# Gates, lengths and the odd value tile's Silu at other places of ScalarE's slot, and the odd value projection ahead of the odd tile's transposition

## The chip, the cores and the metric

One core of a Trainium2 chip runs the whole program. The metric is the device time of one execution in microseconds (us), median of the runs. The engines are TensorE (matmuls; PE, with its weight loads as PEld), VectorE (DVE), ScalarE (ACT), GpSimd (POOL) and SyncE (SP), which only issues DMAs. Each engine runs its own instruction list in order, and they are tied together by semaphores that count up.

## The reference

Four layers over x of 8 x 256 tokens of width 128, each `x = x + f(layernorm(x))`. The first is a gated delta rule with 16 heads, the second a matmul with the signs of a weight, the third a causal attention with 4 key heads, the fourth a mixture of 8 experts with the top 2. The change lies in the first:

```python
q = _causal_conv_silu(x @ Wq.T, conv_q); k = _causal_conv_silu(x @ Wk.T, conv_k)
v = _causal_conv_silu(x @ Wv.T, conv_v)                 # 4 taps, then Silu
q = _l2_norm(q); k = _l2_norm(k)
alpha = exp(-exp(A_log) * softplus(x @ Wa.T + dt_bias)); beta = 2 * sigmoid(x @ Wb.T)
# per token: S = a*(S - b*k k^T S) + k v^T ;  o = S^T q
o = _rms_norm(o).reshape(Bx, Tx, H * DV);  return o @ Wo.T
```

## The kernel before

The recurrence is done in blocks: for each pair of heads and each pair of batches (512 tokens) the decay factors, the products of keys with keys and queries, the inverse of a triangular matrix, and two block solves. There are NN = 32 such steps n (4 parts p of two batches, 8 pairs of heads each). A part needs three things once: the norm of its x, its gates (alpha and beta, from Abs, Exp and Ln on ScalarE) and its lengths (the logarithms of the norms of q and k, split into three bf16 rows for the decay matmul).

The work is laid out by hand as a software pipeline. The loop `for s in range(LAG, NN + LAG + 3)` with LAG = 9 is written out once per engine. One turn s is a slot, and it works on several steps at once: k (projection, taps and Silu of the key and query tiles 2s and 2s+1, only in slots s < 32), g = s - 9 (decays, grams, value tiles 2g and 2g+1), i = s - 10 and j = s - 11 (the two halves of the inverse, then the solves and the output), w = s - 12 (output projection). The last slots also begin the attention. Each engine's order inside a slot is the order of the lines, so a wait holds all that stands behind it on that engine.

The names used here, with the lines of the profile:
- `decay(g, i)` (L531 to L542) writes exponents into bank 2; ScalarE's `exp(g, i)` (L1066) makes `et` of them; `gram(g, i)` (L565) multiplies keys and queries into banks 3 and 1; VectorE's `am` (L1369, L1372) multiplies both, two instructions a gram. A gram must wait until the products of the gram before it are made.
- `inv_a` (L592), `inv_b` (L603), `inv_c` (L610) and `inv_d` (L617) are the inverse's matmuls; `inv_p` (L1394), `inv_y` (L1400, with transpositions L1403 and L1406) and `inv_0` (L1383 to L1390) its steps on VectorE; `inv_n` (L1077), `inv_yf` (L1072, L1073) and `inv_o` (L1083) those on ScalarE. `inv_0` waits for both copies of `inv_yf`.
- `vproj(v)` (L498) projects value tile v, the even one into bank 0, the odd one into bank 2; `vcopy` (L1004, L1009) copies it out, `vconv` (L1293) adds three taps, `vsilu` (L1013) applies Silu, `vtr` (L511) transposes it into bank 0, `vV` (L1023) copies that into V. The even projection waits for the odd tile's vV, since both use bank 0.
- `solve1` (L629), `solve2` (L637), `solve3` (L645) and `out` (L661, L663) are the solves; `u1` (L1089) and `u2` (L1093) copy their results; `ot` (L1099, L1100) squares and copies the outputs. `solve1(j)` waits for `inv_yf(j)` and `inv_o(j)`.
- `kcopy` (L980, L983), `kconv` (L1293), `ksilu` (L990), `ksq` (L996) and `ksel` (L477) make the keys and queries and their squared lengths; `squares` (L672), `rms` (L1416, L1420) and `wout` (L688, L1432) finish a step.
- `gates1` and `gates2` (ScalarE L1028 to L1040, VectorE L1308 to L1332) and `lengths1` to `lengths4` (ScalarE L1044 to L1057, VectorE L1334 to L1356) are the steps of a part. `GAP` says in which slot a norm, a gate matmul or a length matmul is added.
- `exp_ahead` (L1016) is an Exp over one column that nobody reads; in front of it the compiler puts the load of ScalarE's Exp table.
- SyncE: `factors(p)` writes the factors of a part to DRAM, `spread(n)` reads them back over the partitions, `blocks(n)` sends the diagonal blocks through DRAM to GpSimd, `rows(n)` copies the rows of the decay matmul. GpSimd: `substitute` (L1743 to L1751), `scaled` (L1759), a power (L1771).

Of the kernel before, what the change touches and what calls it, by code (L numbers as in the profile page):

```python
# [17 lines left out]
NG = H // GH  # L18
# [3 lines left out]
LAG = 9  # L22
# [7 lines left out]
def program(nc, x_d, wqkv_d, conv_d, wab_d, gate_d, wo_d, sgn_d, awq_d, awk_d, awv_d, awo_d,  # L30
            wr_d, wg_d, wu_d, wd_d, acst_d, ident_d, bmask_d, emask_d, lmask_d, sel_d, reset_d, tri_d, amask_d, out_d):
    with ExitStack() as ctx:
        def sb(name, shape, dt=F32):
            return ctx.enter_context(nc.sbuf_tensor(name, shape, dt))
# [45 lines left out]
        ones = sb("ones", [128, 32])  # L80
        spare = sb("spare", [128, 2])
        ST = sb("ST", [128, 8, 32])
# [151 lines left out]
        for p in range(NP):  # L234
# [5 lines left out]
            if p < NP - 1:  # L240
                GAP[NG * p + 21] = ("norm", ("sg", p))
                GAP[NG * p + 22] = ("signed", p)
        GAP[NN + LAG - 1] = ("norm", ("at", 0))

        def gap(s, kind):
            k, v = GAP[s] if s in GAP else (None, None)
            return v if k == kind else None
# [168 lines left out]
        def _(e):  # L416
# [479 lines left out]
            for s in range(LAG, NN + LAG + 3):  # L896
# [11 lines left out]
                if has_w: squares(w)  # L908
                more(s, 2)
                if has_g: gram(g, 1)  # L910
                if gap(s, "lengths") is not None: lengths(gap(s, "lengths"))
                if gap(s, "gates") is not None: gates(s // NG)
                if gap(s, "norm") is not None: norm(gap(s, "norm"), bank[0], s_vV, 2 * g - 1)
                if gap(s, "signed") is not None: signed_mm(gap(s, "signed"), bank[0], s_vV, 2 * g - 1)
                if has_j: inv_b(j, 1)
                elif j < 0: fill(4)
                more(s, 3)
                if has_g: decay(g, 2)
                if has_g: gram(g, 2)
                if 0 < g < NN: vtr(2 * g - 1)  # L920
                if has_j: inv_c(j)
                elif j < 0: fill(2)
                more(s, 4)
                if has_g: vproj(2 * g)
                if has_j: inv_d(j)
                elif j < 0: fill(2)
                if has_g: vproj(2 * g + 1)
                if has_k and s % NG == NG - 1: ksel(2 * s)
# [36 lines left out]
        def _(e):  # L965
# [32 lines left out]
            def vcopy(v):  # L998
                e.wait_ge(s_vproj, v + 1)
                if v >= 2:  # L1000
                    e.wait_ge(s_vfin, v - 1)
                else:
                    e.wait_ge(s_kfin, NK0)
                e.activation(vy[:, v % 2, :, 3:259], vbank(v)[:, :].rearrange("p (b t) -> p b t", b=2), ACT.Copy).then_inc(s_vcopy, 1)  # L1004
                if v >= 2:
                    e.wait_ge(s_vtr, v - 1)
                else:
                    e.wait_ge(s_ksel, NK0)
                e.activation(vc[:, v % 2, :], vbank(v)[:, :], ACT.Copy, scale=conv[:, 16 + v % 16, 3:4]).then_inc(s_vtap, 1)  # L1009
# [5 lines left out]
            def exp_ahead():  # L1015
                e.activation(spare[:, 1:2], spare[:, 0:1], ACT.Exp)  # L1016

            def vV(v):
# [173 lines left out]
            for s in range(LAG, NN + LAG + 3):  # L1192
# [7 lines left out]
                if g == NN: vV(2 * g - 1)  # L1200
                if has_l: lengths2(p)
                if has_g: exp(g, 1)
                more(s, 0)
                more(s, 1)
                if gap(s, "norm") is not None: norm(gap(s, "norm"))
                if has_l: lengths3(p)
                more(s, 2)
                if has_g: exp(g, 2)
                more(s, 3)
                if has_k: ksilu(2 * s)  # L1210
                if has_k: ksilu(2 * s + 1)
                if 0 < g < NN: vV(2 * g - 1)
                if has_j: inv_n(j)
                if has_j: inv_yf(j)
                more(s, 4)
                if gap(s, "gates") is not None: gates1(s // NG)
                if has_k: ksq(2 * s)
                if has_j: inv_o(j)
                if has_e: ksq(2 * s + 1)
                if has_g: vcopy(2 * g)  # L1220
                if has_k and not has_e: ksq(2 * s + 1)
                if has_g: vcopy(2 * g + 1)
                if has_e: lengths1(s // NG)
                if has_j: u1(j)
                if gap(s, "gates") is not None: gates2(s // NG)
                more(s, 5)
                if has_p: kcopy(2 * s + 2)
                more(s, 6)
                if has_g: vsilu(2 * g)
                if has_p: kcopy(2 * s + 3)  # L1230
                if has_j: u2(j)
                more(s, 7)
                if has_j and j >= NN - 3: ot(j, 0)
                if has_g: vsilu(2 * g + 1)
                if 0 <= g < NN - 1: exp_ahead()
                if has_g: vV(2 * g)
# [10 lines left out]
        def _(e):  # L1247
# [408 lines left out]
            for s in range(LAG, NN + LAG + 3):  # L1656
# [6 lines left out]
                if has_k: kconv(2 * s)  # L1663
                if has_l: lengths2(p)
                if has_j: inv_p(j, 1)
# [3 lines left out]
                more(s, 1)  # L1669
                if has_l: lengths3(p)  # L1670
                if has_k: kconv(2 * s + 1, [0])
# [3 lines left out]
                if has_g: am(g, 3)  # L1675
                if has_l: lengths4(p)
                if gap(s, "gates") is not None: gates1(s // NG)
# [6 lines left out]
                if has_g: am(g, 4)  # L1684
                if has_g: am(g, 5)
                more(s, 4)
                if has_i: inv_0(i)
                if has_w: wout(w, 0)
                if has_e: lengths1(s // NG)
# [7 lines left out]
                more(s, 7)  # L1697
                if LAG < s < NN and s % NG > 2: gates2(s // NG, s % NG - 3)
                if gap(s + 1, "norm") is not None: norm(gap(s + 1, "norm"))
# [173 lines left out]
```

## Time and profile before

| | us |
|---|---|
| median of 3 runs | 1714.56 |
| lowest, highest | 1692.99, 1725.83 |
| the profiled execution | 1699.88 |
| its span | 1697.2 |
| TensorE busy | 1543.7 |
| VectorE busy | 1141.3 |
| ScalarE busy | 850.2 |
| GpSimd busy | 518.9 |
| mean granted TensorE clock | 0.956 of full |

The span runs from the first to the last instruction of one execution; the times of engines are the sums of their instructions in it. They overlap, so they don't add up to the span. The granted clock is a mean over the span of a clock that has two levels, 1.2 and 2.4 GHz.

### The profile page before, as it was taken

To read this page: it belongs to the slowest core of one execution; us is meant where nothing else is said; L and a number is where in the kernel's file an instruction comes from. 1 tells how busy PE (TensorE), PEld (TensorE's weight loads), DVE (VectorE), ACT (ScalarE), POOL (GpSimd) and SP (SyncE) were. 2 spreads that over 40 slices of the span, in tenths; PEclk is the share of its full clock that TensorE was granted. 3 is DMA by queue.
4 is the path that set the end of the run, shared out by engine and by line. 5 is a ranking of instruction groups with operands and counts; after the bars stand their busy time and mean duration, and the time that the engine had idled before them with its cause. 6 is when DMAs were issued, how large, how long until landed. Compare 5 with 4: busy or idle time off the path is not lost.

```text
span 1697.2 us, 32308 instructions
## 1 busy us (share of the span) xinstructions
PE 1543.7 (91%) x12511; PEld 973.3 (57%) x12511; DVE 1141.3 (67%) x2141; ACT 850.2 (50%) x1416; POOL 518.9 (31%) x1019
## 2 busy tenths in 40 slices
PE   5788998989999999999999989888999999899998
PEld 1135676767667666767767765344545445554565
DVE  4837788878888778877767766456547555764533
ACT  6838767676677676665556533222332233222221
POOL 1035657554756355655455430000000000000000
PEclk9879999999999999999999997789999999999999
DMA  3011010101010000010101130000000000000000
GB/s 114 2 27 30 20 26 19 27 16 30 16 24 23 23 22 21 25 22 25 30 19 51 23 145 1 0 1 1 1 1 7 1 1 1 7 0 1 7 1 7
DMA packets 65817, 34.70 MB, mean 20 GB/s; under 512 B 54897, under 2 KB 58225, under 8 KB 65281
## 3 DMA queue, kind: packets, MB, share of 16 engines
q1 hardware_dynamic: 65664, 32.65, 7.1%
q8 instruction: 99, 1.62, 0.4%
q14 instruction: 54, 0.43, 0.1%
HBM read 24.76 MB, written 7.47 MB: 19 GB/s over the span
## 4 chain that ended last, share of the span: by engine, by line
PE 48%; DVE 12%; issue 3%; ACT 3%; DVEq 0%; ACTq 0%
PE bank L867 7%; PE bank L851 6%; PE bank L854 6%; PE bank L565 3%; PE bank L815 3%; PE bank L772 2%; PE bank L798 2%; DVE X L1432 2%; PE bank L661 2%; PE bank L603 2%; DVE vc L1293 1%; PE bank L759 1%; PE bank L775 1%; PE bank L801 1%; PE bank L830 1%
## 5 line engine op out<-in xcount | busy, mean ns | idle before, releaser
L1723 POOL TENSOR_TENSOR st<-st,nh 128x4 f32<-128x4 f32 x16 | 19.2, 1199 | 643.3 <-DVE st L1270 591.0
L1751 POOL TENSOR_TENSOR SU<-SU 128x28 f32<-128x28 f32 (+6 forms) x448 | 200.7, 448 | 35.1
L1747 POOL TENSOR_TENSOR SU<-SU 128x28 f32<-128x28 f32 (+6 forms) x448 | 191.2, 427 | 35.2
L1293 DVE SCALAR_TENSOR_TENSOR vc<-vy,conv,vc 128x512 f32<-128x512 f32 x192 | 145.6, 759 | 14.1 <-ACT vc L1009 9.4
L867 PEld LDWEIGHTS bank<-WQ,AM 128*128 128x128 f32 x1024 | 129.0, 192 | 32.4 <-issue 25.0
L867 PE MATMUL bank<-WQ,AM 128*128 128x128 f32 x1024 | 138.0, 278 | 3.6 <-DVE X L1623 3.6
L851 PE MATMUL bank<-xnT,KQ 128*128 128x512 f32 x256 | 138.5, 623 | 0.0
L854 PE MATMUL bank<-xnT,KQ 128*128 128x512 f32 x256 | 134.4, 607 | 2.1 <-DVE AM L1613 2.1
L1293 DVE SCALAR_TENSOR_TENSOR kc<-ky,conv,kc 128x512 f32<-128x512 f32 x162 | 128.5, 794 | 8.5 <-ACT kc L983 5.1
L1066 ACT ACTIVATE et<-bank 128x512 f32<-128x512 f32 x96 | 57.6, 599 | 126.2 <-PE bank L542 101.6
L1613 DVE TENSOR_TENSOR AM<-bank,qb 128x512 f32<-128x512 f32 x64 | 44.0, 688 | 106.4 <-PE bank L854 83.0
L1171 ACT ACTIVATE qb<-bank 128x512 f32<-128x512 f32 x64 | 38.2, 597 | 149.3 <-PE bank L851 149.3
L1369 DVE TENSOR_TENSOR AM<-bank,et 128x512 f32<-128x512 f32 x128 | 82.3, 684 | 42.7 <-PE bank L565 38.6
L565 PE MATMUL bank<-SM,KQ 64*128 64x128 f32 (+1 forms) x512 | 77.7, 381 | 24.0 <-DVE AM L1369 12.6
L498 PE MATMUL bank<-xnT,WQ 128*128 128x512 f32 x128 | 74.9, 668 | 19.2 <-ACT V L1023 19.2
L1171 ACT ACTIVATE et<-bank 128x512 f32<-128x512 f32 x64 | 38.2, 596 | 102.1 <-PE bank L851 102.1
L854 PEld LDWEIGHTS bank<-xnT,KQ 128*128 128x128 f32 x256 | 50.0, 196 | 66.4 <-issue 63.5
L1383 DVE STREAM_TRANSPOSE PP<-SU 128x512 f32<-128x512 f32 x32 | 34.0, 1062 | 79.9 <-PE bank L617 79.9
L1540 DVE TENSOR_REDUCE SM<-bank 128x2 f32<-128x512 f32 (+1 forms) x96 | 65.3, 685 | 32.9 <-PE bank L775 32.8
L688 PEld LDWEIGHTS bank<-WQ,V 128*128 128x128 f32 x512 | 66.5, 197 | 32.7 <-issue 30.5
L1613 DVE TENSOR_TENSOR AM<-bank,et 128x512 f32<-128x512 f32 x64 | 43.8, 686 | 60.9 <-PE bank L854 34.6
L661 PE MATMUL bank<-AM,U 128*128 128x256 f32 x256 | 81.7, 401 | 2.9 <-ACT V L1100 1.9
(236 smaller groups left out, 3453.0 us busy)
## 6 DMA issues: line engine op xcount, KB each, us to landing
SM<-fscr SPq DMA_DIRECT2D x64, 128.0 KB, 2.9
scratch<-AM SPq DMA_DIRECT2D x128, 48.0 KB, 1.8
SU<-scratch SPq DMA_DIRECT2D x128, 32.0 KB
SM<-SM SPq DMA_DIRECT2D x192, 2.0 KB
WQ<-in_wqkv_dram SPq DMA_DIRECT2D x1, 2048.0 KB, 8.5
KQ<-in_wg_dram SPq DMA_DIRECT2D x4, 512.0 KB, 6.7
KQ<-in_wu_dram SPq DMA_DIRECT2D x4, 512.0 KB, 7.5
WQ<-in_wd_dram SPq DMA_DIRECT2D x1, 2048.0 KB, 13.9
```

The costliest lines, as they stand in the source:

```text
L498: e.matmul(vbank(v)[:, :], wqkv[:, ct * 128:(ct + 1) * 128], xT[:, (n // NG) % 3, :], start=True, stop=True).then_inc(s_vproj, 1)
L565: ins = e.matmul(bank[(3, 1)[hh]][:, part], KQ[hp:hp + 64, m, b, 0, s0:s0 + 128], moved, start=True, stop=True)
L661: e.matmul(b[:, bt * 256:bt * 256 + 256], U[:, hh, 2 * bt, :], AM[:, hh, bt, 512:768], start=True, stop=False, skip_group_check=True)
L851: e.matmul(bank[f % 2][:, :], wg[:, ex, jj * 128:(jj + 1) * 128], x, start=True, stop=True).then_inc(s_g, 1)
L854: e.matmul(bank[2 + f % 2][:, :], wu[:, ex, jj * 128:(jj + 1) * 128], x, start=True, stop=True).then_inc(s_u, 1)
L867: ins = e.matmul(bank[4][:, k * 128:(k + 1) * 128], HB[(4 * d + jj) % 8][:, k * 128:(k + 1) * 128], wd[:, ex, jj, :], start=jj == 0, stop= ...
L1171: e.activation(RG[f % 4], bank[f % 2][:, :], ACT.Relu).then_inc(s_rg, 1)
L1293: e.scalar_tensor_tensor(c, y[:, :, k:k + 256], conv[:, ct, k:k + 1], c, ALU.mult, ALU.add).then_inc(s_c, 1)
L1369: ins = e.tensor_tensor(AM[:, hh, part, :].rearrange("p (c n) -> p c n", c=3)[:, 0:3:2, :], G[:, :].rearrange("p (k t) -> p k t", k=2), E. ...
L1613: e.tensor_tensor(HB[f % 8], bank[2 + f % 2][:, :], RG[f % 4], ALU.mult).then_inc(s_h, 1)
L1747: e.tensor_tensor(tmp[:, :, 0:k, 0:15 - k], sub[:, :, 0:k, k:k + 1].to_broadcast([128, 2, k, 15 - k]), sub[:, :, k:k + 1, k + 1:16].to_bro ...
L1751: e.tensor_tensor(sub[:, :, 0:k, k + 1:16], sub[:, :, 0:k, k + 1:16], tmp[:, :, 0:k, 0:15 - k], ALU.subtract).then_inc(s_su, 1)
```

## The change

TensorE's slot: `inv_b(j, 1)` goes ahead of `gram(g, 1)` and of the added matmuls of norm, gates and lengths; `vproj(2g+1)` goes ahead of `vtr(2g-1)`, and `vtr` behind `inv_c`; `vproj(2g)` becomes the second value projection, behind `inv_d`. The semaphore of the projections counts in that order, and `vcopy` of the even tile waits for both.

ScalarE's slot: `vsilu` of the odd tile is left to the next slot, behind `exp(g, 2)` and a new dummy Silu, and is followed by `inv_n` and `vV`; the two `ksilu` stand behind these. `exp_ahead` moves to behind `vsilu` of the even tile. `gates1` is done one slot after the gate matmul and `gates2` two slots after, both between `exp(g, 1)` and `exp(g, 2)`; `lengths1` comes one slot later, at the same place, with `lengths2` behind it; `lengths3` goes behind `inv_o`. VectorE's halves of the lengths move later in their slot and its five gate steps are spread over slots 4 to 7 of a part by `STEPS_OF`.

```diff
+        STEPS_OF = [(), (), (), (), (0,), (1, 2), (3,), (4,)]
@@ TensorE
                 more(s, 2)
+                if has_j: inv_b(j, 1)
+                elif j < 0: fill(4)
                 if has_g: gram(g, 1)
                 if gap(s, "lengths") is not None: lengths(gap(s, "lengths"))
                 if gap(s, "gates") is not None: gates(s // NG)
...
-                if has_j: inv_b(j, 1)
-                elif j < 0: fill(4)
                 more(s, 3)
                 if has_g: decay(g, 2)
                 if has_g: gram(g, 2)
-                if 0 < g < NN: vtr(2 * g - 1)
                 if has_j: inv_c(j)
                 elif j < 0: fill(2)
+                if has_g: vproj(2 * g + 1)
+                if 0 < g < NN: vtr(2 * g - 1)
                 more(s, 4)
-                if has_g: vproj(2 * g)
                 if has_j: inv_d(j)
                 elif j < 0: fill(2)
-                if has_g: vproj(2 * g + 1)
+                if has_g: vproj(2 * g)
@@ ScalarE
             def vcopy(v):
-                e.wait_ge(s_vproj, v + 1)
+                e.wait_ge(s_vproj, v if v % 2 else v + 2)
...
+            def silu_ahead():
+                e.activation(spare[:, 2:3], spare[:, 0:1], ACT.Silu)
...
-                if has_l: lengths2(p)
                 if has_g: exp(g, 1)
...
-                if has_l: lengths3(p)
+                if gap(s - 1, "gates") is not None: gates1(s // NG)
+                if gap(s - 2, "gates") is not None: gates2(s // NG)
+                if has_l: lengths1(p)
+                if has_l: lengths2(p)
                 more(s, 2)
                 if has_g: exp(g, 2)
                 more(s, 3)
+                if has_k or 0 < g < NN: silu_ahead()
+                if 0 < g < NN: vsilu(2 * g - 1)
+                if has_j: inv_n(j)
+                if 0 < g < NN: vV(2 * g - 1)
                 if has_k: ksilu(2 * s)
                 if has_k: ksilu(2 * s + 1)
-                if 0 < g < NN: vV(2 * g - 1)
-                if has_j: inv_n(j)
                 if has_j: inv_yf(j)
                 more(s, 4)
-                if gap(s, "gates") is not None: gates1(s // NG)
                 if has_k: ksq(2 * s)
                 if has_j: inv_o(j)
+                if has_l: lengths3(p)
...
-                if has_e: lengths1(s // NG)
                 if has_j: u1(j)
-                if gap(s, "gates") is not None: gates2(s // NG)
...
                 if has_g: vsilu(2 * g)
+                if 0 <= g < NN - 1: exp_ahead()
                 if has_p: kcopy(2 * s + 3)
                 if has_j: u2(j)
...
-                if has_g: vsilu(2 * g + 1)
-                if 0 <= g < NN - 1: exp_ahead()
+                if g == NN - 1: vsilu(2 * g + 1)
                 if has_g: vV(2 * g)
@@ VectorE
-                if has_l: lengths2(p)
                 if has_j: inv_p(j, 1)
...
-                if has_l: lengths3(p)
...
                 if has_g: am(g, 3)
-                if has_l: lengths4(p)
+                if has_l: lengths2(p)
...
                 if has_g: am(g, 5)
+                if has_l: lengths3(p)
                 more(s, 4)
                 if has_i: inv_0(i)
+                if has_l: lengths4(p)
...
-                if LAG < s < NN and s % NG > 2: gates2(s // NG, s % NG - 3)
+                for k in STEPS_OF[s % NG] if LAG < s < NN else ():
+                    gates2(s // NG, k)
```

## Rows read from the trace of the kernel before

**Rows 1.** Busy times of the main loop: stretch, length, then each engine, clock, DMA.
```profile
103.00:965.00 862.00, 800.75 (x8696) 577.51 (x8694) 671.77 (x1205) 573.99 (x950) 481.25 (x961) 0.97 0.10 24
```

**Rows 2.** TensorE's waits, 120 to 1000 us: total us, times, longest.
```profile
PE bank L498 <- ACT V L1023: 19.2, 21, 1.5
...
PE bank L565 <- ACT V L1100: 7.9, 7, 1.5
PE bank L629 <- issue: 5.9, 3, 2.9
...
PE bank L637 <- ACT U L1089: 4.3, 3, 2.0
```

**Rows 3.** Timeline of TensorE in a plain slot: start, us, operation, idle before.
```profile
182.01 1.13 PE L498 MATMUL bank<-xnT,WQ 128*128 128x512 f32 x2 [0.88 <-ACT V L1023]
...
201.28 0.64 PE L672 MATMUL bank<-qb,ones 128*32 128x256 f32 x8
202.31 0.70 PE L565 MATMUL bank<-SM,KQ 64*128 64x256 f32 x4 [0.39 <-DVE AM L1369]
...
203.37 1.12 PE L603 MATMUL bank<-YP,PP 64*64 64x32 f32 x32
...
205.07 0.49 PE L565 MATMUL bank<-SM,KQ 64*128 64x128 f32 x4
...
206.16 0.66 PE L511 MATMUL bank<-ident,vc 128*128 128x128 f32 x4
206.75 1.14 PE L610 MATMUL bank<-XP,AM 64*64 64x64 f32 x16
208.77 1.12 PE L498 MATMUL bank<-xnT,WQ 128*128 128x512 f32 x2 [0.88 <-ACT V L1023]
...
212.75 1.06 PE L629 MATMUL bank<-V,YF 128*128 128x128 f32 x8
```

**Rows 4.** Timeline of ScalarE in the same slot.
```profile
205.18 0.60 ACT L1066 ACTIVATE et<-bank 128x512 f32<-128x512 f32 x1 [3.19 <-PE bank L542]
205.79 1.28 ACT L990 ACT_TABLE_LOAD   x1
207.09 1.15 ACT L990 ACTIVATE KQ<-kc 128x512 f32<-128x512 f32 x2
208.15 0.58 ACT L1023 ACTIVATE V<-bank 128x512 f32<-128x512 f32 x1
...
209.36 0.63 ACT L1072 ACTIVATE YF<-YP 64x512 f32<-64x512 f32 x1
...
210.67 0.63 ACT L996 ACTIVATE kc<-KQ 128x512 f32<-128x512 f32 x1
211.32 0.59 ACT L1083 ACTIVATE YF<-bank 64x512 f32<-64x512 f32 x1
```

**Rows 5.** Timeline of VectorE in the same slot.
```profile
203.56 1.29 DVE L1369 TENSOR_TENSOR AM<-bank,et 128x512 f32<-128x512 f32 x2
204.77 0.74 DVE L1293 SCALAR_TENSOR_TENSOR kc<-ky,conv,kc 128x512 f32<-128x512 f32 x1
205.43 0.41 DVE L1400 TENSOR_TENSOR YP<-YP,bank 128x256 f32<-128x256 f32 x1
205.87 0.43 DVE L1406 STREAM_TRANSPOSE XP<-YP 32x256 f32<-32x256 f32 x1
```

**Rows 6.** Timelines of a slot without key work.
```profile
828.98 0.70 PE L565 MATMUL bank<-SM,KQ 64*128 64x256 f32 x4 [0.37 <-DVE AM L1369]
...
836.72 1.05 DVE L1383 STREAM_TRANSPOSE PP<-SU 128x512 f32<-128x512 f32 x1 [2.42 <-PE bank L617]
```

**Rows 7.** Two long waits of TensorE, and a slot's busy times and clock.
```profile
358.84 2.05 PE L629 MATMUL bank<-V,YF 128*128 128x128 f32 x8 [2.86 <-issue]
...
877.63 1.23 PE L565 MATMUL bank<-SM,KQ 64*128 64x256 f32 x4 [1.42 <-ACT V L1100]
...
548.50:580.90 32.40, 32.02 (x294) 22.18 (x293) 24.07 (x40) 18.92 (x32) 17.83 (x33) 0.84 0.08 20
```

More of the change, by code:

```diff
@@ L80, in program @@
         ones = sb("ones", [128, 32])
-        spare = sb("spare", [128, 2])
+        spare = sb("spare", [128, 3])
         ST = sb("ST", [128, 8, 32])
```

## The prediction

> **What bounds the kernel now.** I began with the busy times of the whole main loop: of its 862 us TensorE is busy 801, VectorE 672, ScalarE 574, at a mean granted clock of 0.97 [rows 1]. TensorE sets the pace, and what can move is the 61 us in which it stands idle and the 26 us (862 x 0.03) that the lower clock costs. Then the waits of TensorE: on ScalarE's copy of the odd value tile (vV) 19.2 us in 21 slots, on ScalarE's last copy of outputs (L1100) 7.9 us in 7, ahead of the first solve (L629) 5.9 us in 3, and on U (L637) 4.3 us in 3 [rows 2]. The last three belong to slots that carry a norm, a gate or a length step. Then one plain slot, engine by engine [rows 3 to 5]: from one even value projection to the next it takes 26.76 us, and TensorE idles twice in it: 0.39 ahead of the second gram, until VectorE has its first two products, and 0.88 ahead of the even value projection, until vV is out of bank 0 [rows 3]. At that place ScalarE runs without a gap from the third exp to the copies of the values: table load, two key Silus, vV, inv_n, two YF copies, a square, inv_o [rows 4].
>
> **What the change does to a plain slot** (22 slots with key work, of 31). I replay it on the rows, from the end of the squares at 201.92 (201.28 + 0.64).
>
> *inv_b goes ahead of the second gram.* inv_b takes 1.06 (its 1.12 less an overlap of 0.06 with what follows) and its input is long there. It fills the 0.39. But the gram now begins at 202.98 instead of 202.31 and its last product ends at 204.11. VectorE's third and fourth products began at 203.56, which was when VectorE was free, at the old gram's end; now they wait until 204.26 (0.15 from the end of a gram to VectorE, taken from the first gram) and end at 205.55 [rows 3, 5]. The third gram must wait for them, to 205.61. It began at 205.07, 1.70 behind the start of inv_b, so the decay between takes 0.64, and TensorE would reach the gram at 204.68 (202.98 + 1.06 + 0.64). So 0.39 of idle time goes and 0.93 comes. Behind the products on VectorE stand a key tap (0.66) and inv_y with its transposition (0.44 + 0.43) [rows 5]; they end at 207.00 instead of 206.30. inv_c needs them and now stands directly behind the gram: it starts at 207.04, 0.35 idle.
>
> *vproj(odd) ahead of vtr.* inv_c 1.07, vproj(odd) 1.06 (bank 2, read by the third exp, is free), vtr 0.66: the transposition ends at 209.83 [rows 3]. vsilu of the odd tile stands ready for it: exp at about 204.8, load 1.28, the dummy Silu 0.1, the Silu 0.6, so near 207.4. inv_n has its turn at 208.2. The old wait of vproj(even) for vV does go: vV starts at 209.86, and vproj(even) comes only after inv_d.
>
> *The price stands one step on.* ScalarE is in order, and after vV it still owes two key Silus (1.06), two YF copies (1.31), the first square (0.65) and inv_o (0.59); before, the Silus were done ahead of vV. From vV's start, 209.86: Silus at 210.39 (0.58 less an overlap of 0.05), YF at 211.45, square at 212.76, inv_o from 213.41 to 214.00 [rows 4]. TensorE from vtr's start at 209.17 has 0.59 of it (206.16 to 206.75), then inv_d, a value projection and the first wout, 2.92 together (212.75 less 208.77 and the 1.06 of a projection) [rows 3], and stands at solve1 at 212.68. solve1 reads all of YF, so it waits 1.36 and starts at 214.04, against 212.75 before. That is **+1.3 a plain slot**, 22 x 1.3 = +29. VectorE's inv_0 waits for YF too, but it has room: the rest of the slot keeps its cover.
>
> *Slots without key work* (9). No tap, no key Silu, no square. From the squares' end at 828.61: inv_b 1.06, gram 1.13, 0.15, products 1.29, third gram 1.15, inv_c 1.07, vproj 1.06, vtr 0.66, vV 0.56, YF 1.31, sum 9.44, so inv_0 could start at 838.1; it started at 836.72 [rows 6]. solve1 is not late there, but VectorE is what those slots' inv_b(i, 0) waits for, and it passes the 1.4 on. About 0.1 is saved at the next gram: +1.3, 9 x 1.3 = +12.
>
> *The special steps.* Gates leave the stretch between YF and solve1, lengths1 leaves the place ahead of u1, and vsilu(odd) no longer holds vV and the output copies at the slot's end. The waits of 7.9, 5.9 and 4.3 go: -18. Their new place is ScalarE's gap ahead of the third exp, 3.19 us wide [rows 4]. The first gate half (four steps of 0.6) fits. The second (a load, two Ln, and a load back to Exp) is some 1.2 too long, but vtr leaves it that much room: nothing. The lengths don't fit: Ln, its load, then an Exp that waits for VectorE's step behind the fourth product, then a copy. I make the exp some 3 late there, the odd Silu later than vtr by 1.1, and VectorE's fourth step adds 0.4: +1.5, 3 x 1.5 = +4.5. On SyncE the factors are written later, at about the time when blocks() has its last product anyway, and the rows of the next part have some 5 us until their decay: nothing; if that cover is gone, at most a few us in three slots. Norm slots: VectorE is late for inv_b, +0.35 x 4 = +1.4. Silu and Exp each still load once a plain slot (1.28 [rows 4]): nothing.
>
> Sum: 29 + 12 - 18 + 4.5 + 1.4 = **+29 us**.
>
> **The clock.** It falls to the lower of its two levels now and then: after the 2.86 wait at 358.84 solve1 took 2.05 instead of 1.06, after the 1.42 wait at 877.63 two gram steps took 1.23 instead of 0.70; but one slot ran at 0.84, 5.2 us lost, with no wait over 0.9 near it [rows 3, 7]. Long waits of the old kernel go (at best 26 - 5 = 21 us back), and 31 new ones of about 1.4 come. Ends for this term: -21, and +41 if every fourth of them costs 5.2. I take 0, since most waits of 1.1 to 1.5 between full-size matmuls, where the new one lies, were followed by full clock.
> The Trainium skill ("TensorE: Matmul & The Clock Gate", section "HAM oscillation — how this bites in real kernels") has the clock fall over waits for data clearly longer than these; taken alone it would give the whole 21 back.
>
> **The base.** The profiled execution took 1699.88 us (span 1697.2), 14.7 below the median 1714.56 of three runs that spread over 33. Added to the profiled time the sum gives 1729, added to the median 1744. I forecast **1744**.
>
> **Rivals.** A measurement of this kernel tells about 2% (34 us) from no change.
> - *Forecast*: solve1 waits for inv_o, clock within 15 either way: 1729 to 1759. Chance 0.50, of it 0.27 within 2%, 0.23 slower.
> - *The clock falls at the new waits* (slower): place solve1 and the third gram, 29 + 41: up to 1785. One dip of 5.2 more than before is enough to carry the forecast past 2%. For: [rows 7]. Against: the 0.88 waits of now seldom do. 0.18.
> - *The clock comes back*: 29 - 21, 1723. Against: the 0.84 slot. 0.07, within 2%.
> - *solve1 does not wait*: this needs ScalarE from vV to inv_o to fit in 2.92; by the rows it takes 4.14 (209.86 to 214.00), so only if I have its order or a buffer wrong. Then the slots lose about 0, the special slots give -18 + 6, the clock 0 to -21: 1681 to 1703. 0.15, of it 0.04 faster.
> - *Everything listed goes*: vV 19.2, the 18 of the special slots, the 0.39 waits (31 x 0.39 = 12), and the clock: -49 - 21, 1645. 0.05, faster.
> - *Something late at a part's start* (rows or factors through SyncE): above 1760. 0.05, slower.
>
> **How the numbers follow.** Faster by over 2%: 0.04 + 0.05 = 0.09. Within: 0.27 + 0.07 + 0.11 = 0.45. Slower: 0.23 + 0.18 + 0.05 = 0.46. The range leaves out the last two gains and the end of the clock's case, and takes half of the runs' spread on the lower side: 1697 to 1785. The likeliest case's own range is 1729 to 1759.
>
> **What would show it.** Right: TensorE's waits on vV gone; a new wait at solve1 for YF (L1083's copy) of about 1.4 in each slot with key work; a wait of 0.9 at the third gram; no waits at L637 and none on L1100; plain slots of 28.0 to 28.2; slots without key work at 26.3. Wrong: plain slots at or below 26.8, or no wait at solve1. The total is wrong with right slots if the clock leaves 0.97.

## The result, and the profile after

| | before | changed |
|---|---|---|
| median over the runs of one comparison, us | 1711.53 (12 runs) | 1715.80 (12 runs) |
| lowest, highest | 1692.84, 1725.83 | 1712.31, 1726.42 |
| ratio, 95% interval | | 1.0067, 1.0035 to 1.0100 |
| the profiled execution | 1699.88 | 1712.31 |
| its span, mean granted clock | 1697.2, 0.956 | 1710.5, 0.961 |

By the ratio, the change makes the kernel slower by 0.7% in this comparison, some 11.5 us on 1711.5, and not by the 29 forecast; the two medians are only 4.3 apart. The direction and the new waits are as forecast; the size is not.

Since the granted clock differs from run to run, I split each run's span in two: span times mean granted clock, called the *full-clock part*, and span times (1 - clock), the *clock's loss*. For the kernel before, the first was 1622.6, 1622.6 and 1624.2 us in three comparisons (standard error 0.6, 0.6, 0.5), the second 80.9, 78.8 and 75.3 (about 2). For the changed kernel they are 1640.6 +- 1.1 and 75.2 +- 2.0. The ratios and all means of the two parts are over fast runs, those within 1.5% of the fastest run of the same kernel; over all runs the kernel before comes to 1622.4 to 1623.7 and 82 to 87, which is what the expectations below quote. So the work became about 18 us longer. The loss was 5.7 +- 2.9 us smaller in those runs; a second set of runs, below, does not show that again.

The split has a fault of its own. A stretch at the lower clock that is followed by a wait costs little or nothing, since TensorE would have waited anyway, but the split books half of it as the clock's loss. The slot with the second long wait of L629, in two executions of the kernel before (columns as in [rows 1]):

```profile
580.93:612.43 31.50, 26.33 (x291) 19.05 (x290) 22.59 (x39) 26.50 (x41) 15.51 (x31) 1.00 0.09 21
584.99:616.42 31.43, 27.30 (x291) 19.58 (x289) 22.20 (x39) 26.38 (x41) 16.23 (x32) 0.95 0.08 21
```

It is equally long in both, but its full-clock part is 31.5 in one and 29.7 in the other. So the full-clock part falls as the loss rises: over the 12 runs of the changed kernel by 0.44 +- 0.10 us for each us of loss, over the 23 to 29 of the kernel before by 0.11 to 0.16 (+- 0.04 to 0.06). With the losses 6 us apart, the 18 is to be read as 15 to 18.

The first view is the stretches of the changed kernel: from the third decay of the first step to that of the last (the main loop), and the rest. The columns are those of [rows 1].

```profile
102.60:984.10 881.50, 808.13 (x8692) 584.14 (x8691) 667.10 (x1204) 568.60 (x976) 474.46 (x953) 0.97 0.10 24
984.10:1710.40 726.30, 665.45 (x3630) 373.58 (x3628) 409.79 (x828) 209.55 (x361) 31.46 (x54) 0.96 0.03 11
```

The same two stretches of the kernel before:

```profile
103.10:964.60 861.50, 800.25 (x8692) 577.31 (x8691) 671.40 (x1204) 573.99 (x950) 480.93 (x960) 0.97 0.10 24
964.60:1697.10 732.50, 674.68 (x3630) 377.70 (x3628) 409.19 (x826) 208.61 (x358) 28.80 (x47) 0.95 0.03 11
```

The loop grew by 20.0 us at the same clock in these two executions. The rest has the same matmuls (x3630) in both and is 6.2 shorter in this execution, at a higher clock (0.96 for 0.95).

TensorE's waits in the changed kernel, 120 to 1000 us: total, times, longest. They answer to [rows 2].

```profile
PE bank L612 <- DVE XP L1413: 16.2, 22, 1.5
PE bank L631 <- ACT YF L1088: 16.0, 15, 1.4
PE bank L567 <- DVE AM L1376: 14.7, 23, 0.8
PE bank L605 <- DVE PP L1401: 7.9, 13, 1.0
PE bank L647 <- DVE V L1418: 5.0, 11, 0.9
PE bank L479 <- ACT kc L998: 4.8, 4, 1.4
PE bank L639 <- ACT U L1094: 3.3, 8, 0.4
```

The waits of 19.2 (vV), 7.9 (L1100), 5.9 (L629) and 4.3 (L637) of [rows 2] are gone or small. In their place stand the first solve (L631, L629 before) for YF, the third gram (L567) for VectorE's products, and the third inverse step (L612) for XP.

One plain slot of the changed kernel at full clock (172.5 to 200.7), TensorE: start, us, operation, idle before. It answers to [rows 3].

```profile
173.69 0.49 PE L567 MATMUL bank<-SM,KQ 64*128 64x128 f32 x4 [0.81 <-DVE AM L1376]
...
175.15 1.14 PE L612 MATMUL bank<-XP,AM 64*64 64x64 f32 x16 [0.30 <-DVE XP L1413]
...
177.19 0.60 PE L513 MATMUL bank<-ident,vc 128*128 128x128 f32 x4
...
179.75 1.05 PE L690 MATMUL bank<-WQ,V 128*128 128x128 f32 x8
181.86 1.13 PE L631 MATMUL bank<-V,YF 128*128 128x128 f32 x8 [1.06 <-ACT YF L1088]
182.92 1.50 PE L479 MATMUL bank<-kc,sel 128*16 128x512 f32 x6
184.35 1.16 PE L690 MATMUL bank<-WQ,V 128*128 128x128 f32 x8
```

ScalarE in the same slot, beside [rows 4]:

```profile
176.93 0.59 ACT L1082 ACTIVATE PP<-bank 64x512 f32<-64x512 f32 x1
177.82 0.60 ACT L1028 ACTIVATE V<-bank 128x512 f32<-128x512 f32 x1 [0.30 <-PE bank L513]
178.32 1.14 ACT L992 ACTIVATE KQ<-kc 128x512 f32<-128x512 f32 x2
179.36 0.62 ACT L1077 ACTIVATE YF<-YP 64x512 f32<-64x512 f32 x1
180.00 0.63 ACT L1078 ACTIVATE YF<-YP 64x512 f32<-64x512 f32 x1
180.65 0.63 ACT L998 ACTIVATE kc<-KQ 128x512 f32<-128x512 f32 x1
181.19 0.57 ACT L1088 ACTIVATE YF<-bank 64x512 f32<-64x512 f32 x1
...
182.71 0.62 ACT L998 ACTIVATE kc<-KQ 128x512 f32<-128x512 f32 x1
```

Read together: from vV's start (177.82) to inv_o's end (181.76) ScalarE has no gap, and TensorE, done with `wout` at 180.80, waits until 181.86. The second square (L998) now ends at 183.33, and that is a wait which no bracket of a timeline shows, because it lies inside a group: the six matmuls of L479 began at 182.92 and the next operation at 184.35, 1.43 later. Before, at full clock, the same six (L477) took 0.98 from start to start:

```profile
621.42 1.04 PE L477 MATMUL bank<-kc,sel 128*16 128x512 f32 x6
622.40 1.16 PE L688 MATMUL bank<-WQ,V 128*128 128x128 f32 x8
```

The view of that one source line shows it, with the idle time ahead of each matmul (until what, us, times), 120 to 770 us, first before, then after:

```profile
L477 PE MATMUL bank<-kc,sel x132: 592/602/1036, 136.0 to 733.2; 128*16 128x512 f32 x132
...
  ACT kc L996: 7.8, 11
```

```profile
L479 PE MATMUL bank<-kc,sel x132: 590/593/604, 130.2 to 753.1; 128*16 128x512 f32 x132
...
  ACT kc L998: 21.0, 26
```

Of the 26 idle times after, brackets show four (4.8 us in the list above). From start to start the L479 groups of the 20 slots from this one on take 29.9 us (14 of them 1.43 or 1.44), against 22.0 before (15 of them 0.97 or 0.98): +7.9, of which 0.6 is one slot (its group at 547.68 took 2.03) in which `lengths3`, now behind inv_o, holds the second square up further. The waits that brackets show grew from 60.1 to 72.7 us over the loop, +12.5. The two make 20.4 of the loop's 20.0; small steps elsewhere are 0.4 shorter.

### The profile page after: what moved, and what is told of

Same layout as the page of the kernel before. It is cut to its first block, busy times and chain, and to the rows that moved or that the text cites. A ratio compares the mean times of both kernels' runs of the same rounds, so it can differ in the third digit from the quotient of the medians.

```text
span 1710.5 us, 32336 instructions
## 1 busy us (share of the span) xinstructions
PE 1541.3 (90%) x12511; PEld 975.7 (57%) x12511; DVE 1137.4 (66%) x2141; ACT 845.7 (49%) x1444; POOL 515.1 (30%) x1019
## 4 chain that ended last, share of the span: by engine, by line
PE 66%; DVE 19%; ACT 7%; issue 7%; DMA 0%; POOL 0%; DVEq 0%; SPq 0%; ACTq 0%
PE bank L869 7%; PE bank L853 6%; PE bank L856 6%; PE bank L567 4%; PE bank L605 3%; PE bank L663 3%; PE bank L594 3%; PE bank L500 3%; PE bank L817 3%; DVE kc L1300 2%; PE bank L469 2%; PE bank L612 2%; DVE X L1439 2%; DVE vc L1300 2%; PE bank L479 2%
## 5 line engine op out<-in xcount | busy, mean ns | idle before, releaser
L1731 POOL TENSOR_TENSOR st<-st,nh 128x4 f32<-128x4 f32 x16 | 19.2, 1200 | 657.2 <-DVE st L1277 604.8
L853 PE MATMUL bank<-xnT,KQ 128*128 128x512 f32 x256 | 136.6, 616 | 0.0
L856 PE MATMUL bank<-xnT,KQ 128*128 128x512 f32 x256 | 132.3, 599 | 2.1 <-DVE AM L1620 2.1
L567 PE MATMUL bank<-SM,KQ 64*128 64x128 f32 (+1 forms) x512 | 74.8, 370 | 18.1 <-DVE AM L1376 14.7
L1028 ACT ACTIVATE V<-bank 128x512 f32<-128x512 f32 x64 | 38.2, 597 | 99.3 <-PE bank L513 99.3
L500 PE MATMUL bank<-xnT,WQ 128*128 128x512 f32 x128 | 81.0, 718 | 1.9 <-ACT et L1071 1.8
```

The costliest lines, as they stand in the source:

```text
L500: e.matmul(vbank(v)[:, :], wqkv[:, ct * 128:(ct + 1) * 128], xT[:, (n // NG) % 3, :], start=True, stop=True).then_inc(s_vproj, 1)
L567: ins = e.matmul(bank[(3, 1)[hh]][:, part], KQ[hp:hp + 64, m, b, 0, s0:s0 + 128], moved, start=True, stop=True)
L853: e.matmul(bank[f % 2][:, :], wg[:, ex, jj * 128:(jj + 1) * 128], x, start=True, stop=True).then_inc(s_g, 1)
L856: e.matmul(bank[2 + f % 2][:, :], wu[:, ex, jj * 128:(jj + 1) * 128], x, start=True, stop=True).then_inc(s_u, 1)
```

## The experiments

Every kernel is compared with the kernel before in the same session. The last two columns are means over a kernel's runs less those of the kernel before in that session, with errors of 1 to 2.5 for the first and 2.5 to 6 for the second.

| kernel | median us (runs) | ratio, 95% interval | full-clock part | clock's loss |
|---|---|---|---|---|
| changed | 1715.80 (12) | 1.0067, 1.0035 to 1.0100 | +18.0 | -5.7 |
| changed, again | 1722.18 (6) | 1.0137, 1.0081 to 1.0194 | +16.3 | +4.1 |
| before, again | 1711.38 (12) | 1.0041, 1.0003 to 1.0079 | 0.0 | +6.2 |
| e1 Silus first | 1711.70 (12) | 1.0045, 1.0001 to 1.0090 | +0.7 | +6.1 |
| e2 inv_b back | 1719.47 (6) | 1.0110, 1.0044 to 1.0177 | +19.5 | -2.9 |
| e5 both | 1711.99 (12) | 1.0017, 0.9976 to 1.0059 | +6.2 | -3.5 |
| e3 steps back | 1737.28 (6) | 1.0197, 1.0141 to 1.0253 | +33.2 | -1.3 |
| e4 steps alone | 1719.50 (12) | 1.0071, 1.0032 to 1.0109 | -2.1 | +15.5 |
| e6 swap alone | 1735.11 (6) | 1.0188, 1.0146 to 1.0230 | +22.4 | +10.2 |
| e7 inv_b alone | 1713.13 (12) | 1.0043, 1.0002 to 1.0084 | +4.9 | +2.0 |
| e8 gates alone | 1712.54 (12) | 1.0064, 1.0025 to 1.0103 | -8.3 | +17.5 |
| e9 product later | 1714.71 (12) | 1.0087, 1.0051 to 1.0122 | +16.5 | -3.9 |
| e10 mended | 1713.83 (12) | 1.0076, 1.0040 to 1.0111 | +3.1 | +8.6 |

The changed kernel's own comparison is set here against the first of the three sessions. The third row says how far to trust a ratio: the kernel before against itself came out at 1.0041. The full-clock part repeats within 2 us, so verdicts on mechanisms go by it, with the reserve above: between kernels whose losses lie 15 us apart the split alone can make up a few us.

### The wait at the first solve: the key Silus

```diff
 (changed kernel, ScalarE)
+                if has_k: ksilu(2 * s)
+                if has_k: ksilu(2 * s + 1)
                 if has_j: inv_n(j)
                 if 0 < g < NN: vV(2 * g - 1)
-                if has_k: ksilu(2 * s)
-                if has_k: ksilu(2 * s + 1)
                 if has_j: inv_yf(j)
```

> The changed kernel with the two key Silus of ScalarE put between the odd value tile's Silu and inv_n, instead of behind vV. Theory (ScalarE's backlog behind vV holds solve1): the 15 waits of 1.06 us at solve1 go, 16 us less than the changed kernel, about 0.997 of the kernel before; inv_n starts at the same time since ScalarE stood idle 2.2 us ahead of it. Rival (the clock or VectorE sets those slots): the wait turns up again at the next step, ratio stays at 1.005 to 1.008.

The full-clock part fell from 1640.6 to 1623.3, by 17.3, as the first theory had it, and the wait of L631 for YF, 16.0 us in the changed kernel, was down to one of 0.3. The longest waits were then:

```profile
PE bank L567 <- DVE AM L1376: 14.9, 23, 0.8
PE bank L612 <- DVE XP L1413: 14.8, 21, 1.5
```

So putting two Silus back ahead takes off nearly as much as the change adds at full clock. But the total is a miss: the ratio was to be about 0.997 and is 1.0045, since the clock's loss was 87 here and 75 in the changed kernel.

```diff
 (changed kernel, TensorE)
                 more(s, 2)
-                if has_j: inv_b(j, 1)
-                elif j < 0: fill(4)
                 if has_g: gram(g, 1)
...
                 if gap(s, "signed") is not None: signed_mm(...)
+                if has_j: inv_b(j, 1)
+                elif j < 0: fill(4)
                 more(s, 3)
```

> The changed kernel with inv_b(j, 1) back behind the second gram. Theory (the later gram makes VectorE's products, and with them the third gram and inv_c, late): the 0.81 waits at the third gram and the 0.3 to 0.8 ahead of inv_c go, 0.39 ahead of the second gram comes back, so 0.8 a slot, 22 us less than the changed kernel, about 0.994 of the kernel before, with the wait at solve1 unchanged at about 1.06. Rival (inv_c and vproj only wait longer elsewhere): no more than 5 us.

A miss: 1642.1 against 1640.6, no gain. The waits of the second gram came back, in 31 slots and up to 2.1 long, where norm and signed products of VectorE stand ahead of its first gram product; those of L612 fell only to 7.0, those of L631 stayed:

```profile
PE bank L567 <- DVE AM L1376: 19.1, 31, 2.1
PE bank L631 <- ACT YF L1088: 17.2, 16, 1.4
PE bank L612 <- DVE XP L1413: 7.0, 12, 1.2
```

With both edits at once (e5):

> The changed kernel with both: inv_b back behind the second gram, and the key Silus ahead of inv_n. Theory: the two prices lie on one chain one behind the other and add, 38 us less than the changed kernel, about 0.985 of the kernel before. Rival: they cover each other, and the sum is not more than the larger one, 0.994.

11.8 less than the changed kernel, not 38, and less than the 17.3 of e1 alone, so the rival (no more than the larger one) is the nearer. The second key Silu ahead of `inv_n` makes the fourth inverse step (L619) wait 9.6 us in 17 slots, since without inv_b's 1.06 of cover TensorE is there earlier:

```profile
PE bank L567 <- DVE AM L1376: 19.2, 31, 2.1
PE bank L619 <- ACT PP L1082: 9.6, 17, 0.9
```

### The parts one by one

e6 is the kernel before with the odd Silu, the dummy Silu, the order on ScalarE and that of the value projections as in the change; inv_b, gates and lengths stay:

```diff
 (kernel before)
                 if has_g: gram(g, 2)
-                if 0 < g < NN: vtr(2 * g - 1)
                 if has_j: inv_c(j)
+                if has_g: vproj(2 * g + 1)
+                if 0 < g < NN: vtr(2 * g - 1)
...
-                if has_g: vproj(2 * g)
                 if has_j: inv_d(j)
-                if has_g: vproj(2 * g + 1)
+                if has_g: vproj(2 * g)
 (ScalarE: silu_ahead, vsilu(2g-1), inv_n, vV(2g-1), both ksilu, inv_yf; exp_ahead behind vsilu(2g))
```

> The kernel before with only the odd tile's Silu, the dummy Silu, vV ahead of the key Silus and the two value projections swapped; gates, lengths and inv_b as before. Theory (the price stands at solve1, and in the gate slots it adds to what is there): about 1.3 a slot with key work, 1.015 to 1.022 of the kernel before. Rival (the vV wait of 0.88 that goes pays for it): 0.998 to 1.004.

+22.4 at full clock, and a ratio inside the theory's range: this part is the price.

```profile
PE bank L631 <- ACT YF L1088: 22.6, 14, 4.8
...
PE bank L639 <- ACT U L1094: 7.6, 11, 2.0
```

The 4.8 are two slots (368.39 and 613.74) in which the first gate half still stands ahead of inv_o. inv_b alone (in the kernel before, `inv_b(j, 1)` ahead of `gram(g, 1)`):

> The kernel before with only inv_b(j, 1) ahead of the second gram. Theory: a 0.8 wait at the third gram takes the place of the 0.39 one, and in slots with a norm the wait for VectorE's first products shrinks; plain slots 0.4 longer, norm slots shorter, 1.000 to 1.005. Rival (filling the 0.39 is a gain as such): 0.993 to 0.997.

+4.9, and the ratio of 1.0043 is the theory's: the third gram waits in 20 slots, 0.81 in 15 of them, and the second no longer 0.39.

Gates and lengths: e3 is the changed kernel with them at their old places, e4 the kernel before with them at the new, e8 the kernel before with the gates alone moved.

```diff
 (e8: kernel before, ScalarE; VectorE's gate steps by STEPS_OF as in the change)
+                if gap(s - 1, "gates") is not None: gates1(s // NG)
+                if gap(s - 2, "gates") is not None: gates2(s // NG)
                 if has_l: lengths3(p)
                 more(s, 2)
...
-                if gap(s, "gates") is not None: gates1(s // NG)
...
-                if gap(s, "gates") is not None: gates2(s // NG)
```

> The changed kernel with gates and lengths at their old places on ScalarE and VectorE. Theory (the special steps are where the change gains): the waits at solve1 and u1 in the gate and length slots return, less what the new places cost there, 6 to 12 us more than the changed kernel, 1.010 to 1.014 of the kernel before. Rival (the gain is from the odd tile's Silu no longer holding the outputs): no change against the changed kernel, 1.005 to 1.008.

> The kernel before with only the gates and lengths at their new places on ScalarE and VectorE. Theory (the special steps are where the change gains, whatever the slot's order): the waits of 2.9 at solve1 and 1.2 to 2.0 at u1 go, 10 us, and the clock falls less often: 10 to 22 us less than the kernel before, 0.987 to 0.994. Rival (they gain only where the odd tile's Silu has also been moved): no change, 0.997 to 1.003.

> The kernel before with only the two gate steps moved to where the change has them (the first one slot later, the second two), the lengths at their old places, and nothing of the swap or of the order of the inverse. With gates and lengths moved together the four gate slots gained 3 to 4.7 us each and the three slots that then held two or three lengths lost about 2 each. Theory (the gain is the gates', the loss the lengths'): 9 to 11 us less than the kernel before at full clock (1612 to 1614 against 1622.4), the long waits of the second gate slot and of the output stage gone; ratio 0.993 to 0.996. Rival (fewer waits are answered by a lower clock, as there): the same at full clock, but 8 to 15 us more loss, ratio 1.000 or over.

Taking the moves back costs 15.2 on the changed kernel (1655.8 against 1640.6; 6 to 12 were expected); making them on the kernel before gives 2.1 (10 to 22 expected), of the gates alone 8.3 (9 to 11 expected). So the lengths' moves cost about 6 (8.3 less 2.1), and what the gates' move is worth depends on the rest: with the swap, inv_o is what the solve waits for, and a gate half ahead of it is paid in full (the waits of 4.8 in e6). The waits for U (L637) did not go with the gates. In e8 they are the same in sum as in [rows 2], and those on L1100 even longer (9.7 for 7.9):

```profile
PE bank L498 <- ACT V L1023: 20.7, 21, 1.8
PE bank L565 <- DVE AM L1369: 13.4, 31, 1.2
PE bank L565 <- ACT V L1100: 9.7, 10, 1.5
...
PE bank L637 <- ACT U L1089: 4.3, 3, 2.0
```

The waits for U belong to `lengths1`, which in e8 stands where it stood, ahead of u1. What went with the gates is the wait at L629. And the total did not gain: in e4 and e8, the two kernels with the least work, the clock took 15.5 and 17.5 us more. That is what e8's rival had said; but their ratios (1.0071 and 1.0064) also stand beside the 1.0041 of the kernel before against itself.

### VectorE's late tap

In the slot behind the one shown, the third inverse step waited 1.37, not 0.30. VectorE and GpSimd of the changed kernel at that place:

```profile
201.76 1.82 DVE L1300 SCALAR_TENSOR_TENSOR kc<-ky,conv,kc 128x512 f32<-128x512 f32 x1
203.50 0.41 DVE L1407 TENSOR_TENSOR YP<-YP,bank 128x256 f32<-128x256 f32 x1
203.94 0.43 DVE L1413 STREAM_TRANSPOSE XP<-YP 32x256 f32<-32x256 f32 x1
```

```profile
201.76 1.27 POOL L1767 TENSOR_TENSOR SM<-KQ,SM 128x512 f32<-128x512 f32 x1
```

The tap takes 0.74 in the slot before. In e9 GpSimd's product stands behind the power:

```diff
 (changed kernel, GpSimd)
-                if g + 1 < NN: scaled(g + 1)
                 if w >= 0:
...
                     e.tensor_tensor(RR[:, 1, :, :], ..., ALU.pow)
+                if g + 1 < NN: scaled(g + 1)
```

> The changed kernel with GpSimd's scaled product of the next group (L1767) issued behind the power (L1779) instead of ahead of it. Theory (VectorE's second key tap, L1300, is slowed from 0.74 to 1.3 to 1.8 us because it runs beside the scaled product, and XP and with it the third inverse step are late by that): taps back at about 0.74, the waits of inv_c for XP (16.2 us in 22 in the changed kernel) fall to some 0.3 each, 7 us in all, third gram's waits stay at 0.6 to 0.8; full-clock part 1640.6 - 5 to -9, ratio to the changed kernel 0.995 to 0.998. Rival (the product then meets another VectorE step, or the gram that reads it waits): the waits change places, full-clock part within 3 us of 1640.6 or above it.

```profile
198.52 0.74 DVE L1300 SCALAR_TENSOR_TENSOR kc<-ky,conv,kc 128x512 f32<-128x512 f32 x1
199.18 0.42 DVE L1407 TENSOR_TENSOR YP<-YP,bank 128x256 f32<-128x256 f32 x1
199.63 0.43 DVE L1413 STREAM_TRANSPOSE XP<-YP 32x256 f32<-32x256 f32 x1
200.10 1.81 DVE L1300 SCALAR_TENSOR_TENSOR kc<-ky,conv,kc 128x512 f32<-128x512 f32 x1
```

The mechanism is right: the second tap is back at 0.74, the third inverse step waits 0.30 in all four plain slots, each of which takes 28.20, and the collision (1.81) meets the third tap, for which nobody waits. The gain is a miss: the waits of L612 fell from 16.2 to 11.5 only, and the full-clock part stayed at 1640.7. The two slots with the longest collisions did become 1.0 us shorter in their full-clock part (29.19 to 28.20 and 30.86 to 29.85), and the solve waits 1.05 there as before, so the time did not change places within them. The waits of L631 rose from 16.0 to 17.0 because one slot more waits, which in the changed kernel lay behind a stretch at the lower clock. Of the 11.5 left at L612, 5.0 are waits of 0.96 and 1.53 in four slots with gate or length steps, which are the same in the changed kernel. At a loss of 71.4 for 75.2 the split by itself would put e9 some 1.6 us higher; the rest of the missing gain is not explained.

### A version between the two, and the changed kernel again

```diff
 (kernel before with e6's swap and e8's gates; ScalarE behind vsilu(2g-1))
+                if has_k: ksilu(2 * s)
                 if has_j: inv_n(j)
+                if has_k: ksilu(2 * s + 1)
                 if 0 < g < NN: vV(2 * g - 1)
-                if has_k: ksilu(2 * s)
-                if has_k: ksilu(2 * s + 1)
                 if has_j: inv_yf(j)
```

> The kernel before with the odd value Silu and the odd value projection at the change's places and the gates moved, but with the second inverse step and the lengths at their old places, and ScalarE's order after the value Silu: first key Silu, inv_n, second key Silu, the odd value's copy, YF. So neither both key Silus stand between the copy and YF, nor ahead of inv_n. Theory (the swap's +22.6 us is the solve's wait behind the two key Silus, and one key Silu on each side fits into the cover that is there): waits of the first solve under 5 us in sum, waits of the fourth inverse step under 5, full-clock part about 1615, below the kernel before's 1622.4. Rival (ScalarE's chain from the third inverse step to YF is too long in any order): 1625 to 1635, as with both Silus ahead (1628), with the waits at the fourth step or at the solve.

The waits of L631 for YF went to 0.6, those put down to issue came to 4.3, and those of L619 to 1.6: both under 5, as the theory said, the first only just. But the full-clock part is 1627.3, the rival's. What is left:

```profile
PE bank L567 <- DVE AM L1376: 19.6, 33, 2.1
PE bank L639 <- ACT U L1094: 8.0, 12, 2.0
PE bank L612 <- DVE XP L1413: 7.4, 12, 1.2
...
PE bank L631 <- issue: 4.3, 14, 0.3
```

A plain slot takes 27.15 at best, with 0.72 of bracketed waits, against 26.76 with 1.27: less visible waiting, yet longer. Of it 0.45 is again the late second square inside L479 (1.43 from start to start), and 0.2 each lies ahead of the third inverse step and inside the fourth.

> The changed kernel itself, a second time, to see how much of its ratio and of its clock loss belongs to the kernel. Split of a run's time: span times mean granted clock (the part at full clock) and the rest (the clock's loss). So far the changed kernel stood at 1640.6 +- 1.1 us at full clock and 75.2 +- 2.0 us of loss over 12 runs, the kernel before at 1622.4 and 82 to 87. Theory (the work costs +18 us, and the clock gives some 10 of it back, as a property of the changed kernel): 1640.6 +- 3 again, loss 75 +- 5 again, ratio 1.004 to 1.010. Rival (the loss of a session is a draw): 1640.6 +- 3 again, but a loss of 82 to 87, and a ratio of 1.010 to 1.013.

The full-clock part is 1640.5, as before; the clock's loss is 79.4 +- 4.7 beside the 75.3 +- 1.7 of the kernel before. So here the clock returned nothing, and the ratio is 1.0137, above what both the theory and the rival had said. Between this and the first comparison, whether the changed kernel loses less to the clock is not shown. None of these kernels is faster than the kernel before.

## Why the prediction was wrong in size

- **inv_b ahead of the second gram**: right. Forecast: the third gram waits 0.93 and inv_c 0.35; measured 0.81 and 0.30. inv_c's wait rises to 0.8 to 1.4 where GpSimd's product meets the tap; that was not forecast.
- **vV's wait goes**: right, 19.2 to 0.2.
- **The wait at the first solve**: its mechanism and place are right, and e1 shows it. Its size was off: 1.06 for 1.36, in 15 slots and not 22. One of the 22, the first (at 127.49 in the kernel before), has no solve at all, so its +1.3 should not have been booked. inv_o follows the square by 0.54 (181.19 less 180.65) where I took 0.65, YF follows the Silus 0.10 earlier than their end, and vV starts 0.63 behind vtr, not 0.69. Of the 21 slots with key work and a solve, six others don't wait there: in three, the last of a part, TensorE has just waited 1.42 for the squares, which it reads ahead of the solve there, and in the other three TensorE ran at the lower clock on its way there (297.2 to 307.4, 416.6 to 426.9, 601.0 to 604.4) and came late itself: the wait is 0.0, 0.0 and 0.40. Against that stands what I had left out: the second square is late by the same chain, 0.45 inside `ksel`. So a plain slot became 28.20 (+1.44), inside the forecast 28.0 to 28.2. That it fits so well is luck: one term was too big and one missing, and they cancel.
- **Slots without key work**: a failed step. Forecast +1.3 each, for the eight of them in the loop +10.4, and +1.5 for a length slot among them, less 2.8 for waits on L1100 that end there: +9.1; measured +4.2 (each slot's length less its clock loss, against the same slot before). In the five that ran at full clock in both kernels (starting at 781.41, 806.42, 831.42, 885.74 and 911.82 in the kernel before) it is +0.2, +0.9, +0.9, +0.3 and +0.2. inv_0 came 9.19 behind the squares' end (forecast 9.44), but `inv_b(i, 0)` waits for it no longer than before (0.57), since U and V are waited for ahead of it (0.41 and 0.31). I passed VectorE's whole delay on to TensorE.
- **The special steps**: the other failed step. Forecast -18, and +4.5 for the lengths. Measured in the three slots with a part's first gate half, at full clock in the changed kernel (the last in its second execution): 24.79 to 20.86, 31.33 (with a slow stretch that began inside the wait) to 28.55 and 31.50 to 28.54, so -9.7 in all, where my terms gave -2 (3 x 1.3 less 5.9). e8 shows that the gates do it: with them alone moved, the same slots have full-clock parts of 21.1, 26.8 and 26.8, so 3.7, 4.6 and 4.7 less, where I had booked nothing in the first and the wait of 2.86 in the others. In the first there is no solve; four steps and a table load (131.58 to 135.46) stood on ScalarE ahead of the squares and the copies of the values. In the others the gate half also delayed the second square (L477 took 1.45 and 1.43 from start to start, not 0.98), and in the last a wait of 0.94 for U (L661) goes with it. The lengths cost about 6 (e8 and e4) where I had 4.5.
- **The sum over the loop**, by the split: the 19 other slots with key work +23.9 (my terms, 24.7 + 3.0 + 1.4 less the 9.4 us of waits on L1100 and U that go there: +20), the three with gates -8.7 (-2), the eight without key work +4.2 (+9), the first +0.2: +19.6, where my terms give +27, and the ninth slot without key work and rounding the rest of the 29. Two steps failed by 7 and 5 us on the same side, and the other slots, 4 us over my terms, don't make it good.
- **The clock**: forecast 0, between -21 and +41; measured -5.7 +- 2.9 in one set of runs and +4.1 +- 5.0 in another, so 0 stands. But the first was enough to bring the measured ratio to 1.0067, where the full-clock part alone would give 1640.6 + 80.9 over 1622.6 + 80.9, 1.011, and the second run of the same kernel gave 1.0137. So of the 17 us between the forecast and the 11.5 of the ratio, some 11 are the slots and 6 are a difference of the clock that did not repeat. The rival "the clock falls at the new waits" is not borne out: 15 waits of about 1.06 and 23 of up to 0.81 came, and the mean loss did not rise; the loop's clock was 0.97 in one profiled execution of the changed kernel and 0.96 in the other, 0.97 and 0.98 in those of the kernel before. The rival "the clock comes back" (21 us) is not shown either. The rule that I had set against the trace (the Trainium skill, "TensorE: Matmul & The Clock Gate", section "HAM oscillation — how this bites in real kernels": waits clearly longer than these bring the clock down) would have given all 21 back; e8 speaks against it as a measure, since with the longest wait of [rows 2] gone it lost 17.5 more.

What stays open is what sets the clock's loss of a kernel. It lay between 71 and 94 us for the same matmuls, and no order in it holds: e4 and e8, with the least work, lost most (94 and 93) and changed and e9 least (75 and 71), but by the waits of TensorE in the loop e8 and e1 are alike (57 us each) and lost 93 and 87, while e5 (59) lost 77, e6 (76) 89, and e3, which waited longest (86), 80. In the changed kernel's second profiled execution the part behind the loop, untouched by the change, took 744.4 at 0.94, where the first took 726.3 at 0.96. So the loss is not local to the waits that differ, and no run here isolates its cause.

## What to carry to other kernels

When a wait is removed by letting the late operation go first, follow what was ahead of it to its next reader: here two Silus of 1.06 moved from in front of one copy to in front of another, and a wait of 0.88 became one of 1.06 and a hidden one of 0.45. Look inside grouped operations by their source line, not only at the brackets of a timeline. And where the clock varies, compare span times clock first: it repeated within 2 us where single runs of one kernel lay over 30 us apart. But it is not free of the clock either, since a slow stretch ahead of a wait is booked as a loss that nobody paid; to compare one slot, take it from executions that ran it at full clock.

## What was not expected of the hardware

When VectorE's key tap (two large operands) starts while GpSimd's product (1.27 us, operands in the same memory) is running, it does not slow down in proportion: it ends 0.54 to 0.56 behind the product's end in 11 of 12 meetings in the changed kernel (0.62 in one), whether it then shows 0.74 or 1.82. In the other order the product waits: in e9 a tap began at 320.01 and took its 0.74, and the product that began at 320.11 took 1.76 for 1.26. The Trainium skill ("SBUF — State Buffer", section "Who interferes with whom") says the same: of the two, the one that starts second is blocked until the first is through, and this holds for a VectorE instruction with two inputs there against a GpSimd instruction that reads there. The trace agrees with both halves of it. In the kernel before the same meetings occur (the tap at 318.23 took 1.74), but behind cover.
